# Causal term of the row maxima as row-half products, with new tables of times

## The chip, the cores and the metric

The kernel runs on one core of one Trainium2 chip. The metric is the device time of one execution in microseconds (us); lower is better. The engines are PE (TensorE matmul; PEld is its weight load), DVE (VectorE), ACT (ScalarE), POOL (GpSimd) and SP (the queue that issues DMAs). They run asynchronously and meet at semaphores; each takes its own instructions strictly in program order.

## The reference, cut to what matters

Eight sequences of 512 tokens with 256 channels pass through two layers. Each layer is attention and a feed-forward part, each with layernorms and a residual. Layer 0's attention has 16 heads of 16 channels with rotary positions:

```python
q = apply_rope(split(x @ Wq.T + bq)); k = apply_rope(split(x @ Wk.T + bk)); v = split(x @ Wv.T + bv)
att = jnp.einsum('bhqd,bhkd->bhqk', q, k) / scale
att = jnp.where(tril, att, -jnp.inf)
att = jax.nn.softmax(att, axis=-1)
y = jnp.einsum('bhqk,bhkd->bhqd', att, v) @ Wo.T + bo
...
h = jax.nn.silu(gate) * up            # feed-forward of layer 0, hidden 768
```

Layer 1 has 16 heads of 64 channels, a soft clamp `50 * tanh(sim / 50)` in place of row maxima, and a feed-forward of the form `sigmoid(r) * (relu(k)**2 @ W_v)` on a mix of each token with the one before.

## The kernel before

**Two phases.** `phase1` does layer 0 for all eight sequences, `phase2` layer 1; the last sequence of phase 1 overlaps the first of phase 2. Matrices are kept as a high and a low part of 32-bit words, so most products are three matmuls (`product`, L340).

**The order.** A sequence is cut into pieces ("rope 1", "max 4 0", "exp 3 2"). A dictionary `table` in each phase gives each piece a time in slots; `Schedule` folds times at `SLOTS = 24`: `time // 24` says in which later iteration of the loop the piece runs, and `time % 24` its place in the iteration. Every engine runs those of the pieces that it has a function for, in the order of the places. So one iteration works on up to four sequences at once, and the tables alone decide what stands behind what on each engine. What a piece waits for is written in its function (semaphores). `loading_table`, `prologue_table` and `closing_table` place the weight loads and the pieces around the change of phase. The middle iterations (3 to 6) are a hardware loop; the others are written out.

**Row maxima of layer 0.** The softmax needs each row's maximum ahead of the exponentials. A pair `a` has two heads `e`, one in partitions 0 to 47 and one in 64 to 111 of `qT` and `kT`, so the two heads' products (L901) use the lower and the upper 64 rows of the array. `row_max` on PE computes pair `a` in three units `k`: key tile 3; tiles 2 and 0; tile 1 (`MAX_UNITS`), each into the two banks of a ring `ring_d` of two units. The causal term is then added: for each tile and head one matmul of the 128x128 bf16 identity with `causal` (0 or -1e30), which uses all 128 rows of the array (L905). DVE reduces the unit (L770, "rmax"), PE transposes four heads' maxima (L913, "maxT"), ACT copies them (L698), and SP places them as a 49th row of `qT` (L599, "maxima"). The `score` products (L929) run on 49 rows, also in row halves; their units are two single banks (`ring_s`) which the exponentials (ACT L708) free.

**Rotary chain.** PE "rope" (12 matmuls, L340), DVE "roped" (L761, L763), POOL "rope_sum" (L638), ACT "rope_hi" (L686), POOL "rope_lo" (L642), and then SP "place" (L592), six DMAs for each of four parts, which bring `roped` to `kT` or `qT`. "max 0 0" waits for places 0 and 1, "max 4 0" for 2 and 3. POOL also masks the probabilities ("mask", L216 and three L221) and forms low halves ("hidden_lo", L655).

**End of layer 0's attention.** "o" (PE), "o_out", "o_stats" and "o_norm" with the residual add (DVE L802, L316, L332, L815), "x1_stats", POOL "x1_rstd" (L328), DVE "x1_norm" (L332), and PE "x1_T" (L963), from which the feed-forward's gate and up products start.

**Phase 2.** PE's larger units alternate between the two halves of `ring_s` there: ... score 4 2, qk 6, r, key, score 5 0 ... A "qk" unit is read by ACT "qk_hi" (L1344) and then DVE "qk_lo" (L1424), which frees it; "r" is read and freed by ACT "r_out" (L1381). "key" takes the unit that "qk 6" held. Layer 1's probabilities are freed through "tanh" (ACT L1354). "den" and "recip" (DVE L1433) are the softmax denominators, "o" adds a pair into the output (L1589).

The places are floats. In phase 2 "r_out" stands at 40.48 and "qk_hi 6" at 16.48:

```python
self.order = sorted(times, key=lambda piece: times[piece] % length)
```

Of the kernel before, what the change touches and what calls it, by code (L numbers as in the profile page):

```python
# [66 lines left out]
class Schedule:  # L67
# [28 lines left out]
    def tail(self, length):  # L96

        return [(j * length + self.place[piece], piece, j - self.shift[piece]) for j in range(BATCH, self.last + 1)
                for piece in self.order if self.present(j, piece)]
# [256 lines left out]
def phase1(nc, block, ctx, memory, a, x_mid, tok, banks, psum, ident, expo):  # L356
# [40 lines left out]
    causal = sb("causal", [P, P], BF16)  # L397
    identb = sb("identb", [P, P], BF16)
# [14 lines left out]
    with nc.sbuf_tensor("l0_staging", [P, 2 * NM, T], F32, side="right") as raw:  # L413
# [30 lines left out]
        "maxT_out": {(0,): 7.28, (1,): 12.62, (2,): 18.46, (3,): 23.86},
        "maxima": {(0,): 8.17, (1,): 18.03, (2,): 21.23, (3,): 26.53},
        "pv": {(0,): 15.68, (1,): 21.44, (2,): 29.89, (3,): 33.35},
        "pv_out": {(0,): 15.89, (1,): 23.68, (2,): 29.21, (3,): 31.18},
        "outT": {(0,): 19.01, (1,): 24.9, (2,): 32.26, (3,): 33.65},
        "outT_norm": {(0,): 19.04, (1,): 24.56, (2,): 30.73, (3,): 33.23},
        "att_T": {(0,): 33.79, (1,): 34.01},  # L450
        "att_T_hi": {(0,): 33.24, (1,): 33.42},
        "att_T_lo": {(0,): 33.44, (1,): 33.6},
        "o": {(0,): 35.78, (1,): 35.99},
        "o_out": {(0,): 34.28, (1,): 34.92},
        "x1_T": {(0,): 40.07, (1,): 41.01},
        "x1_T_hi": {(0,): 39.85, (1,): 40.46},
        "x1_T_lo": {(0,): 40.83, (1,): 42.16},
        "o_stats": {(): 35.25},
# [1199 lines left out]
```

## Time and profile before

| | us |
|---|---|
| median of 3 runs (1732.78 to 1738.29) | 1736.45 |
| profiled execution | 1738.71 |
| its span, first to last instruction | 1737.0 |
| PE busy | 1556.6 |
| DVE / ACT / POOL busy | 1065.2 / 834.8 / 827.8 |
| mean granted TensorE clock, share of full | 0.932 |

Phase 2's first matmuls on PE stand at 797.4 us; in steady state an iteration of phase 1 takes 93.6 to 94.9 us and one of phase 2 some 106.3 us. A matmul's start is the number to trust: ends are modelled, so its cost is the distance from its start to the next one's. At 2.4 GHz 128 columns stream in 53 ns, 256 in 107 ns and 512 in 213 ns. The granted clock is 1.00 (2.4 GHz) or 0.50 (1.2 GHz).

### The profile page before, as it was taken

The page shows a single profiled execution, that of the slowest core. Times are in us where ns is not written, and L with a number is a line of the kernel's source. Part 1 is how long each engine was busy: PE and PEld are TensorE (multiplying, and loading weights), DVE is VectorE, ACT ScalarE, POOL GpSimd, SP SyncE. Part 2 cuts the span into 40 slices and gives each one's busy share as a digit, 9 for nine tenths or more (in the row PEclk, how much of TensorE's full clock was granted, in tenths as well). Part 3 has the DMA queues.
Part 4 walks back from the last instruction along what each step waited for, and adds up shares of the span by engine and source line. Part 5 has one row for each costly group of instructions (what it writes and reads, how often), then busy time and mean ns, then how long its engine had stood idle before and what let it go on. Part 6 is the DMA issues. An engine that isn't in the chain of part 4 may idle for free.

```text
span 1737.0 us, 28461 instructions
## 1 busy us (share of the span) xinstructions
PE 1556.6 (90%) x10528; PEld 1109.1 (64%) x10528; DVE 1065.2 (61%) x1796; ACT 834.8 (48%) x1205; POOL 827.8 (48%) x1007
## 2 busy tenths in 40 slices
PE   2788999999898999898999999999999999999963
PEld 2445675756666666666777677676776767767643
DVE  3557576676757676675565577565674656747562
ACT  2233444343433434364555566655666556655531
POOL 2132343334343424342455655766566556675552
PEclk9677999989999989998999999999999999999986
DMA  6433332222233332311010001010000100000000
GB/s 143 62 50 50 49 62 50 37 46 47 43 49 61 49 61 37 62 62 61 25 47 8 1 2 37 1 38 1 8 28 0 36 0 27 9 1 25 1 25 12
DMA packets 46768, 61.31 MB, mean 35 GB/s; under 512 B 4928, under 2 KB 31968, under 8 KB 46688
## 3 DMA queue, kind: packets, MB, share of 16 engines
q1 hardware_dynamic: 45824, 59.56, 16.9%
q8 instruction: 53, 0.87, 0.2%
q10 hardware_dynamic: 864, 0.66, 0.1%
q14 instruction: 27, 0.22, 0.1%
HBM read 26.35 MB, written 8.39 MB: 20 GB/s over the span
## 4 chain that ended last, share of the span: by engine, by line
PE 75%; ACT 5%; issue 5%; DVE 5%; POOL 4%; DMA 4%; SPq 2%; POOLq 0%; ACTq 0%; DVEq 0%
PE psum L340 36%; PE psum L1573 8%; PE psum L1548 7%; PE psum L1589 5%; PE psum L943 4%; PE psum L929 4%; PE psum L1561 4%; DMA l_qT<-l_roped_hi 2%; PE psum L901 2%; SPq L592 2%; PE psum L905 2%; ACT l_probs L708 2%; ACT l_probs L1354 1%; PE psum L963 1%; POOL l_roped_lo L642 1%
## 5 line engine op out<-in xcount | busy, mean ns | idle before, releaser
L708 ACT ACTIVATE l_probs<-psum 128x512 f32<-128x512 f32 (+1 forms) x384 | 181.0, 524 | 291.0 <-PE psum L929 290.3
L1433 DVE RECIPROCAL l_att<-psum 128x512 f32<-128x512 f32 x64 | 214.5, 3352 | 62.8 <-PE psum L1561 60.7
L770 DVE TENSOR_REDUCE l_rowmax<-psum 128x2 f32<-128x1024 f32 (+3 forms) x256 | 203.0, 819 | 79.9 <-PE psum L905 78.8
L1354 ACT ACTIVATE l_probs<-psum 128x1024 f32<-128x1024 f32 (+1 forms) x192 | 165.0, 879 | 112.5 <-PE psum L1548 84.3
L1424 DVE TENSOR_TENSOR l_qk_lo<-psum,l_qk_hi 128x1024 fp32r<-128x1024 f32 x64 | 78.0, 1220 | 200.6 <-ACT l_qk_hi L1344 200.6
L221 POOL TENSOR_SCALAR_AFFINE_SELECT l_probs<-l_probs 128x256 f32<-128x256 f32 (+1 forms) x384 | 182.6, 507 | 0.0
L216 POOL TENSOR_TENSOR l_pool_holder<-expo 128x1 f32<-128x1 f32 x128 | 28.8, 225 | 292.5 <-ACT l_probs L708 183.2
L1360 ACT ACTIVATE l_probs<-l_probs 128x2048 f32<-128x2048 f32 (+1 forms) x128 | 160.8, 1269 | 1.6
L1573 PE MATMUL psum<-l_probs,l_v 128*64 128x512 f32 (+3 forms) x1024 | 150.4, 436 | 0.9 <-DVE l_att L1439 0.9
L1573 PEld LDWEIGHTS psum<-l_probs,l_v 128*64 128x64 f32 x1024 | 71.1, 137 | 89.6 <-issue 78.6
L929 PE MATMUL psum<-l_qT,l_kT 49*128 49x512 f32 (+3 forms) x512 | 100.8, 432 | 30.6 <-ACT l_probs L708 24.9
L1288 POOL TENSOR_TENSOR l_keysum<-l_probs 128x768 f32<-128x768 f32 x64 | 118.0, 1844 | 6.3
L901 PE MATMUL psum<-l_kT,l_qT 48*128 48x512 f32 (+3 forms) x512 | 86.9, 378 | 33.4 <-DMA l_qT<-l_roped_hi 26.6
L1296 POOL TENSOR_TENSOR l_attT_lo<-l_att,l_attT_hi 128x512 fp32r<-128x512 f32 x64 | 87.8, 1377 | 51.5 <-ACT l_attT_hi L1372 51.5
L328 POOL TENSOR_TENSOR l_x_rstd<-l_x_veps,expo 128x4 f32<-128x4 f32 x48 | 49.7, 1035 | 125.3 <-DVE l_x_veps L322 124.5
L655 POOL TENSOR_TENSOR l_hT_lo<-l_gated,l_hT_hi 128x512 fp32r<-128x512 f32 x48 | 61.5, 1282 | 98.9 <-ACT l_hT_hi L722 98.7
L638 POOL TENSOR_TENSOR l_roped_lo<-l_straight,l_turned 128x512 f32<-128x512 f32 x32 | 41.0, 1280 | 132.7 <-DVE l_turned L763 126.9
L1344 ACT ACTIVATE l_qk_hi<-psum 128x1024 fp32r<-128x1024 f32 x64 | 65.7, 1026 | 79.3 <-PE psum L340 78.9
L1548 PE MATMUL psum<-l_qk_hi 64*128 64x512 f32 (+3 forms) x512 | 97.6, 376 | 4.9 <-DVE l_qk_lo L1424 1.6
L943 PE MATMUL psum<-l_probs,l_v 128*32 128x512 f32 (+3 forms) x1024 | 92.5, 510 | 1.9 <-ACT l_probs L708 1.2
L929 PEld LDWEIGHTS psum<-l_qT,l_kT 49*128 49x128 f32 x512 | 47.2, 201 | 73.0 <-ACT l_probs L708 31.0
L901 PEld LDWEIGHTS psum<-l_kT,l_qT 48*128 48x128 f32 x512 | 51.2, 213 | 56.5 <-issue 44.4
(193 smaller groups left out, 4253.6 us busy)
## 6 DMA issues: line engine op xcount, KB each, us to landing
l_kT<-l_roped_hi SPq DMA_DIRECT2D x64, 128.0 KB, 4.0
l_qT<-l_roped_hi SPq DMA_DIRECT2D x64, 128.0 KB, 5.1
l_xin<-in_x SPq DMA_DIRECT2D x8, 512.0 KB, 4.2
l_kT<-l_roped_lo SPq DMA_DIRECT2D x32, 128.0 KB, 5.1
l_qT<-l_roped_lo SPq DMA_DIRECT2D x32, 128.0 KB, 4.7
l_x<-in_x SPq DMA_DIRECT2D x8, 512.0 KB, 4.0
x_mid<-l_x SPq DMA_DIRECT2D x8, 512.0 KB, 5.3
l_xin<-x_mid SPq DMA_DIRECT2D x8, 512.0 KB, 4.1
```

The source lines that it names most:

```text
L221: nc.gpsimd.affine_select(out=part, in_=part, compare_op=ALU.is_ge, fill=0.0, base=0, pattern=[[0, part.shape[1]], [1, P]], channel_multip ...
L340: last = nc.tensor.matmul(out, l(c), r(c), start=(k == 0), stop=(k == len(todo) - 1))
L708: ring_s.free(nc.scalar.activation(probs[:, SLOT[p], e, c0:c1], ring_s.unit(*use)[:, 0:c1 - c0], ACT.Exp, scale=HD0 ** -0.5), *use)
L770: reduced = nc.vector.tensor_reduce(rowmax[:, t, a // 2, :, a % 2], ring_d.unit("max", a, k)[:, :, c0:c0 + (t + 1) * P], mybir.AxisListTyp ...
L901: nc.tensor.matmul(unit[:, e, c0:c0 + (t + 1) * P], qT[rows, a, t * P:(t + 1) * P], kT[rows, a, 0:(t + 1) * P], start=(c0 == 0), stop=False)
L929: last = nc.tensor.matmul(ring_s.unit("score", p, u, e)[:, c0:c0 + T - kt * P], kT[rows, p, kt * P:(kt + 1) * P], qT[rows, p, kt * P:T], s ...
L943: last = nc.tensor.matmul(ring_d.unit("pv", g)[32 * j:32 * j + 32, 0, kt * P:T], v0[:, kt, h * VSTEP:h * VSTEP + 32], probs[:, SLOT[p], j ...
L1354: ring_s.free(nc.scalar.activation(probs[:, p % 2, :, c0:c1], ring_s.unit("score", p, u)[:, :, 0:c1 - c0], ACT.Tanh, scale=HD1 ** -0.5 / C ...
L1360: nc.scalar.activation(part, part, ACT.Exp, scale=CLAMP).then_inc(exped.sem, 1)
L1433: ring_d.free(nc.vector.reciprocal(att[p % 2][:], ring_d.unit("den", p)), "den", p)
L1548: last = nc.tensor.matmul(ring_s.unit("score", p, u)[:, e, c0:c0 + T - kt * P], l[half, slot, 1, kt * P:(kt + 1) * P], r[half, slot, 0, kt ...
L1573: last = nc.tensor.matmul(ring_d.unit("pv", p)[64 * e:64 * e + 64, kt * P:T], v1[:, kt, 2 * p + e, :], probs[:, p % 2, e, OFF1[kt]:OFF1[kt ...
```

## The change

1. The causal term of a tile and head is now two products of 64 rows each. Head `e` uses the row half of the array in which its own product runs. For `h = 0` the operands are the first 64 rows' selector and 128 columns, for `h = 1` the second 64 rows' selector and the last 64 columns only (the first 64 hold zeros there). The constants are `later` and `rows_of` in place of `causal` and `identb`, and POOL builds them with some more small operations at the start, which PE waits for.
2. All tables have new times, so pieces stand in another order on every engine, in both phases, and at the start and the change of phase.
3. Places are rounded to three decimals when compared, so that equal places count as equal.

```diff
-        self.order = sorted(times, key=lambda piece: times[piece] % length)
-        self.place = {piece: time % length for piece, time in times.items()}
+        self.place = {piece: round(time % length, 3) for piece, time in times.items()}
+        self.order = sorted(times, key=self.place.get)
...
-        for eye in (ident, identb):
...
+        for h in range(2):
+            eye = rows_of[:, h, ROW0 * h:ROW0 * h + ROW0]
+            nc.gpsimd.affine_select(out=eye, in_=eye, compare_op=ALU.not_equal, fill=1.0, base=0,
+                                    pattern=[[-1, ROW0]], channel_multiplier=1).then_inc(consts, 1)
+        nc.gpsimd.affine_select(out=later[:], in_=later[:], compare_op=ALU.is_ge, fill=MASKED, base=-ROW0,
+                                pattern=[[-1, P]], channel_multiplier=1).then_inc(consts, 1)
...
             for t, c0 in MAX_UNITS[k]:
-                for e in range(2):
-                    last = nc.tensor.matmul(unit[:, e, c0 + t * P:c0 + (t + 1) * P], identb[:], causal[:],
-                                            start=False, stop=(t == MAX_UNITS[k][-1][0]))
+                for h in range(2):
+                    for e in range(2):
+                        rows = slice(ROW0 * e, ROW0 * e + ROW0)
+                        c1 = c0 + t * P
+                        last = nc.tensor.matmul(unit[:, e, c1 + ROW0 * h:c1 + P], rows_of[rows, h, :], later[rows, 0:P - ROW0 * h],
+                                                start=False, stop=(t == MAX_UNITS[k][-1][0] and h == 1))
...
-        "rope_lo": {(0,): -5.62, (1,): -1.8, (2,): 0.82, (3,): 9.75},
+        "rope_lo": {(0,): -8.13, (1,): -4.93, (2,): 7.35, (3,): 11.37},
```

PE, where the written-out first iteration computes maxima (`l_kT,l_qT` is the product of queries and keys, L901 before and L913 after). Before:

```order
L901 MATMUL psum<-l_kT,l_qT 128x512 x2
L905 MATMUL psum<-l_causal,l_identb 128x128 x2
L901 MATMUL psum<-l_kT,l_qT 128x384 x2
L901 MATMUL psum<-l_kT,l_qT 128x128 x2
L905 MATMUL psum<-l_causal,l_identb 128x128 x4
```

After:

```order
L913 MATMUL psum<-l_kT,l_qT 128x512 x2
L920 MATMUL psum<-l_later,l_rows_of 128x128 x2
L920 MATMUL psum<-l_later,l_rows_of 128x64 x2
L913 MATMUL psum<-l_kT,l_qT 128x384 x2
L913 MATMUL psum<-l_kT,l_qT 128x128 x2
L920 MATMUL psum<-l_later,l_rows_of 128x128 x2
```

Each pair of full-array matmuls became two pairs in row halves, 64 columns shorter in all, and nothing between the two heads' products uses the full array.

POOL in the loop of phase 1, from the end of "rope_sum 0" on (L638 and L650 are "rope_sum", L642 and L654 "rope_lo", L216 and L221 the masks, L655 and L667 "hidden_lo"; REGISTER_ALU and ISA rows are its waits and loop counters). Before, from behind mask 2:

```order
L150 REGISTER_ALU
L216 TENSOR_TENSOR l_pool_holder<-expo 128x1
L221 AFFINE_SELECT l_probs<-l_probs 128x4x128
L221 AFFINE_SELECT l_probs<-l_probs 128x2x128 x2
L641 ISA
L642 TENSOR_TENSOR l_roped_lo<-l_roped_lo,l_roped_hi 128x512
L654 ISA
L655 TENSOR_TENSOR l_hT_lo<-l_gated,l_hT_hi 128x512
L150 REGISTER_ALU
L638 TENSOR_TENSOR l_roped_lo<-l_straight,l_turned 128x512
L641 REGISTER_ALU
L642 TENSOR_TENSOR l_roped_lo<-l_roped_lo,l_roped_hi 128x512
```

After, from behind mask 2:

```order
L653 ISA
L654 TENSOR_TENSOR l_roped_lo<-l_roped_lo,l_roped_hi 128x512
L150 REGISTER_ALU
L650 TENSOR_TENSOR l_roped_lo<-l_straight,l_turned 128x512
L653 REGISTER_ALU
L654 TENSOR_TENSOR l_roped_lo<-l_roped_lo,l_roped_hi 128x512
L150 REGISTER_ALU
L216 TENSOR_TENSOR l_pool_holder<-expo 128x1
L221 AFFINE_SELECT l_probs<-l_probs 128x4x128
L221 AFFINE_SELECT l_probs<-l_probs 128x2x128 x2
L666 ISA
L667 TENSOR_TENSOR l_hT_lo<-l_gated,l_hT_hi 128x512
```

"mask 3" and "hidden_lo 0" moved from ahead of "rope_sum 1" and "rope_lo 1" to behind them.

ACT in phase 2 (L1360 and L1375 are the exponentials, L1381 and L1396 "r_out", L1344 and L1359 "qk_hi 6"). Before:

```order
L1360 ACTIVATE l_probs<-l_probs 128x2x1024
L1354 ACTIVATE l_probs<-psum 128x2x256
L1360 ACTIVATE l_probs<-l_probs 128x2x256
L1381 ACTIVATE l_sig_r<-psum 128x1024
L1344 ACTIVATE l_qk_hi<-psum 128x1024
L1395 ACTIVATE l_dx<-psum 128x1024
```

After:

```order
L1369 ACTIVATE l_probs<-psum 128x2x256
L1375 ACTIVATE l_probs<-l_probs 128x2x1024
L1359 ACTIVATE l_qk_hi<-psum 128x1024
L1375 ACTIVATE l_probs<-l_probs 128x2x256
L1396 ACTIVATE l_sig_r<-psum 128x1024
L1410 ACTIVATE l_dx<-psum 128x1024
```

"qk_hi 6" stood behind "r_out" and now stands ahead of it. Other orders of which the prediction speaks, as piece names: on PE of phase 1 "o 0, o 1, score 0 2, score 1 0, max 4 0, maxT 1, score 1 1, score 1 2, max 4 1, score 2 0, max 4 2, pv 0, max 5 0, x1_T 0" became "o 0, score 0 2, o 1, max 4 0, score 1 0, maxT 1, max 4 1, score 1 1, score 1 2, score 2 0, max 4 2, max 5 0, pv 0, x1_T 0"; on DVE there "rmax 4 1, x1_stats, rmax 4 2" became "rmax 4 1, rmax 4 2, x1_stats"; ahead of it "x2_norm, rmax 3 2, outT_norm 3" became "outT_norm 3, x2_norm, rmax 3 2". "gate 3" moved from ahead of "max 0 0" on PE to behind it. On DVE of phase 2 "qk_lo 1, recip 6" became "recip 6, qk_lo 1".

## Rows read from the trace of the kernel before

**Rows 1.** The page, part 1: busy us (share of the span) xinstructions.
```profile
PE 1556.6 (90%) x10528; PEld 1109.1 (64%) x10528; DVE 1065.2 (61%) x1796; ACT 834.8 (48%) x1205; POOL 827.8 (48%) x1007
```

**Rows 2.** Waits of PE: who waited <- for whom: us in total, times, longest.
```profile
PE psum L901 <- DMA l_qT<-l_roped_hi: 26.6, 7, 12.5
...
PE psum L340 <- DVE l_qk_lo L1424: 23.0, 7, 3.3
```

**Rows 3.** Windows of phases 1 and 2: us, busy times, PEclk, DMA share, GB/s.
```profile
0.00:797.30 797.30, 695.25 (x4752) 474.84 (x4753) 504.06 (x1009) 310.54 (x618) 282.67 (x413) 0.90 0.31 57
797.30:1683.20 885.90, 846.62 (x5710) 621.00 (x5708) 541.54 (x735) 516.56 (x579) 534.38 (x587) 0.98 0.05 17
```

**Rows 4.** Timeline, PE, phase 1: start us, us, instruction, count.
```profile
311.08 0.29 PE L905 MATMUL psum<-l_causal,l_identb 128*128 128x128 bf16 x2
311.29 0.50 PE L929 MATMUL psum<-l_qT,l_kT 49*128 49x512 f32 x2
311.63 0.40 PE L901 MATMUL psum<-l_kT,l_qT 48*128 48x384 f32 x4
311.97 0.40 PE L905 MATMUL psum<-l_causal,l_identb 128*128 128x128 bf16 x4
312.17 0.47 PE L340 MATMUL psum<-l_yT_hi,l_wgu_hi 128*128 128x512 f32 x1
312.49 0.39 PE L340 MATMUL psum<-l_yT_lo,l_wgu_hi 128*128 128x512 f32 x1
```

**Rows 5.** Timeline, PE, phase 2: 64-row pairs of 128 columns.
```profile
1088.07 0.27 PE L1548 MATMUL psum<-l_qk_lo,l_qk_hi 64*128 64x128 f32 x2
1088.18 0.28 PE L1548 MATMUL psum<-l_qk_hi,l_qk_lo 64*128 64x128 f32 x2
```

**Rows 6.** Timeline, 471 to 492 us: POOL, SP's queue and PE.
```profile
471.32 1.35 POOL L221 TENSOR_SCALAR_AFFINE_SELECT l_probs<-l_probs 128x512 f32<-128x512 f32 x3
...
479.45 1.27 POOL L638 TENSOR_TENSOR l_roped_lo<-l_straight,l_turned 128x512 f32<-128x512 f32 x1
481.46 1.29 POOL L642 TENSOR_TENSOR l_roped_lo<-l_roped_lo,l_roped_hi 128x512 fp32r<-128x512 f32 x1 [0.74 <-ACT l_roped_hi L686]
...
485.31 1.24 SPq L592 DMA_DIRECT2D l_qT<-l_roped_hi  x2
...
491.58 0.50 PE L901 MATMUL psum<-l_kT,l_qT 48*128 48x512 f32 x2 [2.14 <-DMA l_qT<-l_roped_hi]
```

**Rows 7.** Windows of one iteration of phase 1.
```profile
440.90:456.70 15.80, 12.63 (x96) 7.45 (x94) 13.58 (x38) 6.15 (x14) 5.01 (x10) 0.78 0.33 77
...
492.50:499.30 6.80, 6.80 (x24) 4.67 (x22) 2.94 (x4) 1.09 (x2) 0.00 (x0) 0.50 0.00 0
```

**Rows 8.** Timeline, DVE and PE, phase 1, around x1_norm and x1_T.
```profile
454.04 0.69 DVE L770 TENSOR_REDUCE l_rowmax<-psum 128x2 f32<-128x512 f32 x1
455.25 1.38 DVE L332 TENSOR_SCALAR l_gated<-l_x,l_x_mv,l_x_rstd 128x256 f32<-128x256 f32 x4 [0.51 <-POOL l_x_rstd L328]
...
456.68 0.55 PE L963 MATMUL psum<-ident,l_gated 128*128 128x128 f32 x3
```

**Rows 9.** Timeline, PE, ACT and DVE, phase 2, around the r and key products.
```profile
1093.71 0.28 PE L340 MATMUL psum<-l_wrkv_hi,l_mixr_hi 128*128 128x256 f32 x1
...
1096.71 1.02 ACT L1381 ACTIVATE l_sig_r<-psum 128x1024 f32<-128x1024 f32 x1 [2.63 <-PE psum L340]
1097.63 1.02 ACT L1344 ACTIVATE l_qk_hi<-psum 128x1024 fp32r<-128x1024 f32 x1
...
1098.68 1.22 DVE L1424 TENSOR_TENSOR l_qk_lo<-psum,l_qk_hi 128x1024 fp32r<-128x1024 f32 x1 [8.95 <-ACT l_qk_hi L1344]
...
1099.96 0.71 PE L340 MATMUL psum<-l_mixk_hi,l_wrkv_hi 128*128 128x512 f32 x1 [3.29 <-DVE l_qk_lo L1424]
```

**Rows 10.** Window in phase 2 behind such a wait.
```profile
994.30:997.70 3.40, 3.40 (x10) 2.66 (x9) 0.00 (x0) 0.00 (x0) 3.05 (x3) 0.50 0.01 2
```

**Rows 11.** The page, part 5: busy, mean ns | idle before.
```profile
L1433 DVE RECIPROCAL l_att<-psum 128x512 f32<-128x512 f32 x64 | 214.5, 3352 | 62.8 <-PE psum L1561 60.7
```

More of the change, by code:

```diff
@@ L96, in tail @@
     def tail(self, length):
-        return [(j * length + self.place[piece], piece, j - self.shift[piece]) for j in range(BATCH, self.last + 1)
+        return [(round(j * length + self.place[piece], 3), piece, j - self.shift[piece]) for j in range(BATCH, self.last + 1)
                 for piece in self.order if self.present(j, piece)]
@@ L444, in phase1 @@
[L444 to L458, printed above, removed]
-        "o_rstd": {(): 36.56},
-        "residual": {(): 38.86},
-        "o_norm": {(): 36.73},
-        "x1_stats": {(): 37.93},
-        "x1_rstd": {(): 38.53},
-        "x1_norm": {(): 39.85},
@@ new lines, in phase1 @@
+        "outT_norm": {(0,): 19.48, (1,): 26.58, (2,): 29.43, (3,): 32.25},
+        "att_T": {(0,): 34.44, (1,): 34.91},
+        "att_T_hi": {(0,): 34.22, (1,): 34.27},
+        "att_T_lo": {(0,): 33.91, (1,): 34.01},
+        "o": {(0,): 35.92, (1,): 36.13},
+        "o_out": {(0,): 35.03, (1,): 35.9},
+        "x1_T": {(0,): 40.2, (1,): 40.82},
+        "x1_T_hi": {(0,): 40.73, (1,): 41.84},
+        "x1_T_lo": {(0,): 40.66, (1,): 41.21},
+        "o_stats": {(): 36.14},
+        "o_rstd": {(): 37.27},
@@ new lines, in phase1 @@
+        "residual": {(): 36.14},
+        "o_norm": {(): 36.23},
+        "x1_stats": {(): 37.12},
+        "x1_rstd": {(): 38.61},
+        "x1_norm": {(): 40.18},
+        "gate": {(0,): 41.86, (1,): 43.76, (2,): 47.77, (3,): 49.04, (4,): 50.8, (5,): 52.38},
+        "tanh": {(0,): 43.53, (1,): 46, (2,): 47.98, (3,): 48.46, (4,): 51.47, (5,): 54.61},
+        "gated": {(0,): 43.67, (1,): 44.96, (2,): 48.09, (3,): 50.92, (4,): 52.12, (5,): 53.01},
+        "up": {(0,): 42.82, (1,): 44.58, (2,): 48.63, (3,): 50.4, (4,): 51.73, (5,): 53.54},
@@ L499, in start @@
     def start(pieces):
-        timed = sorted([*times.items(), *loading.items()], key=lambda entry: entry[1] % SLOTS)
+        timed = sorted([*times.items(), *loading.items()], key=lambda entry: round(entry[1] % SLOTS, 3))
         for piece, _ in timed:
@@ L1116, in phase2 @@
[L1116 to L1125 removed]
+        "load_x": {(): -15.66},
+        "x_stats": {(): -17.44},
+        "x_rstd": {(): -16.12},
+        "x_norm": {(): -4.47},
+        "x_T": {(0,): -2.88, (1,): -2.61},
+        "x_T_hi": {(0,): -1.68, (1,): -1.05},
@@ L1126, in phase2 @@
+        "mix_lo": {(0,): 37.82, (1,): 38.28},
+        "r": {(): 41.13},
+        "r_out": {(): 40.72},
+        "key": {(): 41.73},
+        "key_out": {(): 41.26},
+        "square": {(): 43.59},
+        "kact_hi": {(): 44.18},
+        "kact_lo": {(): 47.02},
+        "out": {(): 44.93},
+        "out_out": {(): 46.29},
+        "gate": {(): 45.21},
+        "x4_stats": {(): 47.67},
+        "x4_rstd": {(): 52.11},
+        "x4_norm": {(): 52.53},
+        "store": {(): 49.62},
     }
```

251 lines of the change are left out of this document (119 added, 132 removed).

## The prediction

> **What bounds the kernel now.** I read the page's busy times first [rows 1]: PE is busy for 90% of the span, the next engine, DVE, for 61%. So I asked in which stretches PE is not the limit. The windows by phase [rows 3] say: phase 1 has PE busy for 695 of 797 us at a mean clock of 0.90, phase 2 for 847 of 886 us at 0.98. There is thus some slack in phase 1, and next to none in phase 2 beyond single waits. The waits of PE [rows 2] name two that the change of order touches: 26.6 us for the DMAs that place the rotated queries (12.5 us of it once, at the start) and 23.0 us, in seven waits of 3.3 us, for DVE's "qk_lo" of phase 2. The rest of the time PE works, so matmuls that get cheaper count nearly in full, unless another chain sets the end of the stretch in which they stand.
>
> **The causal products.** The timeline of PE [rows 4] prices them from start to start. Four L905 with 128 columns take 0.20 us (311.97 to 312.17), 0.05 us each, which is just their columns. What surrounds them costs more. Going from the row halves to the full array: the four L901 at 311.63 have 512 columns in all (0.213 us) and the next starts 0.34 us later, 0.13 us extra; I use 0.11, since not every such step comes out as dear. Going back: the two L905 at 311.08 need 0.107 us, the next starts 0.21 us later, 0.10 us extra. The first 32-bit pair after such a change is late once more: 311.29 to 311.63 is 0.34 us for 512 columns (0.213 us), 0.12 us extra. A full-array product behind L905 pays only on its first step: 312.17 to 312.49 is 0.32 us, 0.10 us over its columns.
>
> An iteration of phase 1 has 24 maximum units with 32 tiles. Before: 24 entries at 0.11 (2.6 us), 64 matmuls at 0.053 (3.4 us), 11 units followed by another row-half product at 0.22 (2.4 us), 13 followed by something else at 0.10 (1.3 us); 9.7 us. After: entry is free. The new pairs run in no row of this trace. Their lower bound is a bf16 step of the full array, 0.055 us a pair (the two heads run at once, as L901's do); the upper bound is the nearest pair in row halves, 32-bit and 128 columns, 0.11 us [rows 5]. I take 0.055 us, since the weights are bf16 like L905's: 64 pairs, 3.5 us. The 64-column pair gets no more than that credit, since four instructions stand behind each pair. In the new order 13 units are followed by row halves (0.09 us each for the next pair's 32-bit weights, 1.2 us) and 11 by something else (now a change, 0.21 us each, 2.3 us). Sum 7.0 us. The new order also has six more changes elsewhere (score products cut in between full-array ones): 6 x 0.21 = 1.3 us. Net gain 1.4 us an iteration, 11 us over eight. Four of the 24 units stand in a stretch that PE does not end (below), so I book **-10 us**. At 0.11 us a pair this term would be +17 us.
>
> The Trainium skill, "TensorEngine Tiling (Array Packing)", section Instruction Overhead, states about 60 cycles of overhead for each matmul and the same latency for 1 column as for 60. That speaks against the change: with 64 matmuls more in an iteration it would be an estimate of 0.025 us x 64 x 8 = 13 us more, and the term +3 instead of -10. The rows show no such overhead on four L905 in a row, so my sum goes without it.
>
> **The wait at "max 0 0".** Without the 12.5 us at the start it is 26.6 - 12.5 = 14.1 us in six waits [rows 2], one an iteration from the third sequence on. The timeline [rows 6] shows the chain: POOL does mask 3 (471.32) and hidden_lo 0 before rope_sum 1 at 479.45, and rope_lo 1 ends at 482.75; then six DMAs leave, the last pair from 485.31; PE goes on at 491.58, 6.3 us later, after 2.14 us of waiting, so it was there at 489.4. In the new order rope_sum 1 and rope_lo 1 stand right behind rope_lo 0. Input for rope_sum 1 was ready by 466.4; with rope_lo 0 at some 469.7 the pair is done at about 473.5. SP then becomes the limit: maxima 2 and twelve DMAs at 0.62 us from about 471.5 end at 480; the last pair then leaves at 478.8, and with the same 6.3 us it has landed by 485.1. PE arrives 1.4 us earlier than now ("gate 3" has moved behind, its work is only postponed) and about 1 us earlier through cheaper masks: 487. The wait goes, with 2 us to spare: **-12 us**, leaving 2 for iterations where it does not.
>
> **The clock behind it.** After this wait the granted clock is 0.50 for 3.4 or 6.8 us, with PE busy all the time [rows 7]; over these six places 23.9 us ran at 1.2 GHz, which costs half of that, 12 us. Without the idle time before it I expect most of it back: **-9 us**.
>
> **What gets worse in phase 1.** From o 0 to x1_T 0 (440.90 to 456.68) PE is busy for 12.6 of 15.8 us, at a mean clock of 0.78, and DVE for 13.6 [rows 7]. x1_norm ends at 456.6 and x1_T starts at 456.68 [rows 8]: the norm chain through DVE sets this stretch, PE only just keeps up. The new order makes that chain longer: o 1 comes behind score 0 2 and two changes of mode (0.5 us), and rmax 4 2 (0.69 us [rows 8]) ahead of x1_stats: +1.2 us. The same stretch starts earlier, because outT_norm 3 no longer waits behind x2_norm and rmax 3 2: the wait of 0.9 us ahead of att_T goes, 0.7 us net. Sum +0.5 us in seven iterations: **+3.5 us**. PE will stand idle ahead of x1_T instead of ahead of scores, and the clock drop there stays; it costs nothing while the norms are late.
>
> **The wait at "key" in phase 2.** [rows 9]: qk 6 has ended at 1093.71 when r starts. ACT takes r_out first, at 1096.71, and only at 1097.63 qk_hi 6; qk_lo 6 follows at 1098.68, ends at 1099.90, and key starts at 1099.96, after 3.29 us of waiting. The tables tie here (16.48 twice) and the float remainder decides. In the new order qk_hi 6 stands ahead of r_out. ACT is free by then (tanh 4 2 and the exponential fit into the 4.2 us of o 0 and qk 6), so qk_hi 6 and qk_lo 6 take 1.02 + 1.22 us from 1093.71, done at 1096.1, before r's last matmul at 1096.5. The wait is gone, seven times: **-23 us**. What is late next is "out", whose operands come 1 us before PE by my walk through the chain key, square, kact.
>
> Behind each of these waits the clock falls to 0.50 for 3.4 us (once 6.8) [rows 10], 27.3 us in all, 13.6 us lost. No other drop stands in phase 2's steady state. **-12 us**.
>
> **What gets worse in phase 2.** Its new order has 38 changes of array mode instead of 35 in an iteration: 3 x 0.21 x 7 = **+4.4 us**. And DVE does recip 6 (3.35 us [rows 11]) before qk_lo 1 (1.22 us): 4.7 us from den 6's end until score 0 1 may start, against 4.1 us of PE's work in between (o 4, pv 6, score 0 0, den 7): 0.6 us; x3_T comes 0.8 us closer to the norm that it waits for: at most as much again. 1.2 x 7: **+8 us**. The start and the last 54 us keep their chains: 0. POOL's extra constants (eight small operations of 0.3 us) fit into its 11.5 us of idle time before x_rstd; without that cover they would cost 2 us once.
>
> **Sum.** -10 - 12 - 9 + 3.5 - 23 - 12 + 4.4 + 8 = -50 us, against 1738.7 us of the profiled execution: 1688.6. That execution is 2.3 us over the median of the runs: 1686. I forecast 1685 us.
>
> **Rivals.** *Only phase 2 gains (14 in 100).* For it: phase 1 has 100 us of slack on PE, and the norm chain may set more of an iteration than the one stretch. Then -23 - 12 + 12 = -23 us: 1713. *Row-half pairs go at the pace of 32-bit weights (10 in 100).* For it: the only 64-row rows [rows 5]; against it: bf16 L905 at 0.05. 27 us more than the forecast: 1712. *The wait at key goes elsewhere (6 in 100):* DVE or POOL, 60% busy, come late at den or score by as much; phase 1's -27 stays: 1709 to 1720. *Nothing of the order's gains comes (4 in 100):* both waits are replaced, and the masks' gain pays for the added changes: within 5 us of before. *Slower: half-filled arrays do not hold the clock (5 in 100).* The causal products were the only full-array work inside the runs of maxima and scores. If PE's clock stays at 1.2 GHz through these runs, an iteration of phase 1 would have some 20 us more at half speed, 10 us lost, 80 us in all against the 50 gained: 1765. It decides from 12 us more at half clock in an iteration. Against it: scores and L901 run at full clock between 456.7 and 489.4.
>
> **The numbers.** The forecast itself has 61 in 100, with its own range of 1664 to 1702: phase 2's +8 may be 0, the clock may come back in full and the masks be dearer or cheaper by 10. The range to 1714 takes in the first three rivals in part and leaves out about 2 in 10. A change under 0.3% (5 us) can't be told from none. Faster 0.90, same 0.04, slower 0.06.
>
> **What would show it.** In the changed profile: no wait of PE for "qk_lo" ahead of key and no 0.50 clock behind it; an iteration of phase 2 near 102.5 us; no DMA wait at max 0 0; an idle PE of 2 to 4 us ahead of x1_T; L920 pairs 0.05 to 0.06 us apart; an iteration of phase 1 near 90.5 us. I am wrong if L920 pairs stand 0.1 us apart, if the windows of phase 1 show more half clock, or if a new wait of over 2 us stands in each iteration.

## The result, and the profile after

The changed kernel takes 1665.47 us (median of 4 runs, 1663.48 to 1669.93) against 1737.37 us; the ratio of the means is 0.9594, 95% interval [0.9567, 0.9621]. The forecast was 1685 us with a range of 1662 to 1714, and faster at 90 in 100. So the direction and the range hold, though the time stands only 3.5 us above the range's lower end, and the gain is 72 us where 51 were forecast (profiled execution against profiled execution: 1666.4 against 1738.7, and 1688.6 forecast). The missing 22 us are the subject below.

The page's busy times of the changed kernel, as in [rows 1]:

```profile
PE 1517.2 (91%) x11040; PEld 1090.6 (66%) x11040; DVE 1068.6 (64%) x1796; ACT 833.4 (50%) x1205; POOL 834.3 (50%) x1012
```

PE has 512 matmuls more and 39 us less busy time. Its waits (who waited <- for whom, us in total, times, longest), as in [rows 2]:

```profile
PE psum L944 <- ACT l_probs L720: 23.5, 26, 1.2
...
PE psum L913 <- DMA l_qT<-l_roped_hi: 12.5, 1, 12.5
...
PE psum L913 <- DVE l_rowmax L782: 9.7, 12, 1.7
```

Of the seven DMA waits of [rows 2] only the first one, at the start, is left, and the wait for "qk_lo" ahead of key has gone from the list. The waits of the maximum products for DVE's reductions have grown from 2.3 us to 9.7. The windows, as in [rows 3], with phase 2 now starting at 757.7 us, and the last row the closing chain:

```profile
0.00:757.70 757.70, 666.75 (x5265) 464.55 (x5266) 500.45 (x1009) 312.75 (x618) 285.36 (x418) 0.92 0.34 60
757.70:1610.50 852.80, 835.44 (x5709) 612.50 (x5707) 548.61 (x735) 513.02 (x578) 538.24 (x587) 0.99 0.06 18
1610.50:1664.60 54.10, 15.03 (x69) 13.58 (x68) 19.55 (x52) 7.68 (x9) 10.72 (x8) 0.59 0.04 15
```

Phase 1 ends 39.6 us earlier (797.3 to 757.7; the forecast's terms for it sum to -27.5), and what follows is 32.8 us shorter (forecast -22.6). An iteration of phase 1 takes 88.5 to 88.8 us from x1_T to x1_T (92.1 to 95.1 in the kernel before, measured the same way; forecast near 90.5), one of phase 2 102.0 from key to key (forecast near 102.5).

The timeline of PE where a row-half causal term stands between other row-half products, as in [rows 4]:

```profile
383.87 0.50 PE L913 MATMUL psum<-l_kT,l_qT 48*128 48x512 f32 x2
384.22 0.26 PE L920 MATMUL psum<-l_later,l_rows_of 64*128 64x128 bf16 x4
384.31 0.48 PE L944 MATMUL psum<-l_qT,l_kT 49*128 49x512 f32 x2
384.63 0.40 PE L913 MATMUL psum<-l_kT,l_qT 48*128 48x384 f32 x4
```

The four L920 of a tile (a pair of 128 columns and a pair of 64) take 0.09 us from start to start (384.22 to 384.31), and 192 columns stream in 0.080. So a tile costs less than the 0.11 us of the forecast and far less than the 0.22 of its upper bound. The next pair of 512 columns takes 0.32 us (384.31 to 384.63), 0.11 us over its columns: that part of the step back to 32-bit operands stayed, as the forecast had it (0.09). The Trainium skill's "TensorEngine Tiling (Array Packing)", section Instruction Overhead, states some 60 cycles of overhead for each matmul. Taken as time that each matmul adds, as in the prediction's estimate, the trace does not agree: 192 columns leave 0.01 us over, for two pairs. Taken as the least time of a matmul, as in the section's example (1 column takes as long as 60), these rows say nothing of it, since both products have more columns than that.

Around key in phase 2, as in [rows 9] (PE, ACT and DVE):

```profile
1047.18 0.28 PE L340 MATMUL psum<-l_wrkv_hi,l_mixr_hi 128*128 128x256 f32 x1
...
1047.38 1.03 ACT L1359 ACTIVATE l_qk_hi<-psum 128x1024 fp32r<-128x1024 f32 x1
...
1048.44 1.23 DVE L1439 TENSOR_TENSOR l_qk_lo<-psum,l_qk_hi 128x1024 fp32r<-128x1024 f32 x1 [5.70 <-ACT l_qk_hi L1359]
...
1049.98 0.40 PE L340 MATMUL psum<-l_mixk_hi,l_wrkv_hi 128*128 128x512 f32 x1
```

qk_hi 6 starts 0.2 us after r, qk_lo 6 ends at 1049.67, and key starts at 1049.98 without a wait.

### The profile page after: what moved, and what is told of

Same layout as the page of the kernel before. It is cut to its first block, busy times and chain, and to the rows that moved or that the text cites. A ratio compares the mean times of both kernels' runs of the same rounds, so it can differ in the third digit from the quotient of the medians.

```text
span 1664.6 us, 29499 instructions
## 1 busy us (share of the span) xinstructions
PE 1517.2 (91%) x11040; PEld 1090.6 (66%) x11040; DVE 1068.6 (64%) x1796; ACT 833.4 (50%) x1205; POOL 834.3 (50%) x1012
## 4 chain that ended last, share of the span: by engine, by line
PE 83%; DVE 8%; ACT 3%; issue 2%; POOL 2%; DMA 2%; SPq 1%; POOLq 0%; DVEq 0%; ACTq 0%
PE psum L340 41%; PE psum L1588 8%; PE psum L1563 8%; PE psum L1604 5%; PE psum L958 5%; PE psum L1576 4%; PE psum L944 4%; PE psum L913 3%; DVE l_rowmax L782 2%; PE psum L920 1%; ACT l_probs L1369 1%; PE psum L978 1%; ACT l_probs L720 1%; PE psum L967 1%; PE psum L928 1%
## 5 line engine op out<-in xcount | busy, mean ns | idle before, releaser
L221 POOL TENSOR_SCALAR_AFFINE_SELECT l_probs<-l_probs 128x256 f32<-128x256 f32 (+1 forms) x384 | 180.6, 502 | 0.0
L1375 ACT ACTIVATE l_probs<-l_probs 128x2048 f32<-128x2048 f32 (+1 forms) x128 | 160.1, 1270 | 1.3
L216 POOL TENSOR_TENSOR l_pool_holder<-expo 128x1 f32<-128x1 f32 x128 | 29.2, 228 | 243.3 <-ACT l_probs L720 121.8
L1311 POOL TENSOR_TENSOR l_attT_lo<-l_att,l_attT_hi 128x512 fp32r<-128x512 f32 x64 | 93.7, 1469 | 61.4 <-ACT l_attT_hi L1387 61.2
L944 PE MATMUL psum<-l_qT,l_kT 49*128 49x512 f32 (+3 forms) x512 | 96.8, 415 | 25.7 <-ACT l_probs L720 23.5
L913 PE MATMUL psum<-l_kT,l_qT 48*128 48x512 f32 (+3 forms) x512 | 88.0, 384 | 27.7 <-DMA l_qT<-l_roped_hi 12.5
L667 POOL TENSOR_TENSOR l_hT_lo<-l_gated,l_hT_hi 128x512 fp32r<-128x512 f32 x48 | 61.8, 1287 | 90.0 <-ACT l_hT_hi L734 90.0
L650 POOL TENSOR_TENSOR l_roped_lo<-l_straight,l_turned 128x512 f32<-128x512 f32 x32 | 41.1, 1285 | 130.7 <-DVE l_turned L775 125.0
L1359 ACT ACTIVATE l_qk_hi<-psum 128x1024 fp32r<-128x1024 f32 x64 | 65.8, 1028 | 77.1 <-PE psum L340 77.1
L913 PEld LDWEIGHTS psum<-l_kT,l_qT 48*128 48x128 f32 x512 | 50.6, 207 | 54.2 <-issue 32.4
L1305 POOL TENSOR_TENSOR l_keysum<-l_keysum,l_probs 128x512 f32<-128x512 f32 x64 | 83.4, 1303 | 5.0
```

The lines of the kernel that those rows point to most:

```text
L221: nc.gpsimd.affine_select(out=part, in_=part, compare_op=ALU.is_ge, fill=0.0, base=0, pattern=[[0, part.shape[1]], [1, P]], channel_multip ...
L913: nc.tensor.matmul(unit[:, e, c0:c0 + (t + 1) * P], qT[rows, a, t * P:(t + 1) * P], kT[rows, a, 0:(t + 1) * P], start=(c0 == 0), stop=False)
L944: last = nc.tensor.matmul(ring_s.unit("score", p, u, e)[:, c0:c0 + T - kt * P], kT[rows, p, kt * P:(kt + 1) * P], qT[rows, p, kt * P:T], s ...
L1375: nc.scalar.activation(part, part, ACT.Exp, scale=CLAMP).then_inc(exped.sem, 1)
```

## The experiments

Times are medians of 5 or 6 runs; the kernel before had medians of 1737.4 to 1738.2 us beside them. The changed kernel was not run again beside them; differences to it are differences to its median of 1665.5 us.

**One tie undone.** The kernel before, one number changed.

```diff
-        "qk_hi": {..., (5,): 14.69, (6,): 16.48, (7,): 20.03},
+        "qk_hi": {..., (5,): 14.69, (6,): 16.47, (7,): 20.03},
```

> The kernel before, with one place of phase 2 changed: qk_hi 6 at 16.47 instead of 16.48, so that ACT takes it ahead of r_out. My theory: this one swap is the whole of phase 2's gain. The seven waits of 3.29 us ahead of key go and with them the seven drops of the clock behind them (23.8 us at half, 12 us lost): 33 to 38 us less than before, some 1700 us, and a key-to-key distance of 101.4 us instead of 106.3. Rival: the gain of phase 2 needs the whole new order; the swap alone moves the wait to out or to the scores behind it and brings 5 to 15 us.

1703.2 us, ratio 0.9796 [0.9775, 0.9816]: 34.3 us less, as the theory had it (33 to 38; the terms were 23 + 12). Windows of one iteration and of the whole of phase 2's middle:

```profile
1092.50:1193.79 101.29, 100.82 (x702) 73.75 (x701) 66.55 (x92) 63.97 (x71) 66.78 (x73) 1.00 0.05 17
821.30:1598.59 777.29, 771.32 (x5293) 566.03 (x5293) 496.67 (x670) 482.75 (x540) 499.50 (x548) 1.00 0.05 17
```

The clock is 1.00 over 777 us. Nearly half of what the change brings comes from a tie in the table that a float remainder had decided the wrong way.

**The tie put back.** The changed kernel with "qk_hi 6" at 16.73, behind "r_out" (16.72).

> The changed kernel with one place of phase 2 moved: qk_hi 6 behind r_out, as before. Theory: the wait of 3.3 us ahead of key comes back in each of the seven iterations, and behind it 3.4 us at half clock: +33 to +38 us over the changed kernel (1700). Rival: in the new order another piece covers it, +0 to +12 us; or the wait comes back but the clock stays up, since nothing else in the iteration waits: +23 us.

1696.7 us, 31 us over the changed kernel, just under the theory's 33 to 38. The wait of 3.29 us is back seven times, but the drop of the clock only four times: none stands behind the first, the second and the last wait. Windows behind the second, the fourth, the fifth and the last of these waits:

```profile
1054.65:1058.10 3.45, 3.45 (x18) 2.59 (x20) 0.00 (x0) 0.35 (x1) 3.18 (x3) 1.00 0.00 0
1268.22:1271.60 3.38, 3.38 (x8) 2.73 (x9) 0.00 (x0) 0.00 (x0) 3.14 (x4) 0.51 0.00 0
1375.26:1380.70 5.44, 5.44 (x14) 3.86 (x14) 0.00 (x0) 0.00 (x0) 3.81 (x3) 0.50 0.00 0
1590.60:1594.00 3.40, 3.40 (x18) 2.56 (x20) 0.00 (x0) 0.32 (x1) 3.18 (x3) 1.00 0.00 0
```

**Row-half causal products alone.** The kernel before with the change's part 1, all orders as they were.

> The kernel before with the row-half causal products (and their constants) alone, all orders as before. Theory: the products are cheaper by themselves. By the prediction's terms 2.7 us an iteration without the six extra changes of mode (9.7 to 7.0), less what falls where PE doesn't set the end: -18 us. With the pair spacings that the changed kernel's trace shows (67 ns for 128 columns, 28 for 64, nothing extra behind them) 3.5 us an iteration: -25 us. The DMA wait at max 0 0 stays at about 2 us or grows, since PE arrives earlier. Rival A: the earlier arrival of PE at its waits swallows the gain: 0 to -8 us. Rival B: more instructions cost more than they save: +3 to +13 us.

1723.1 us, ratio 0.9913 [0.9899, 0.9926]: -14.4 us, between the theory's 18 and rival A's 8, and well short of the 25 that the pair spacings gave.

**Full-array products in the new order**, the reverse: the changed kernel with the causal term as before.

> The changed kernel with the causal term as before (full-array identity times causal), in the new order. Theory: as in the old order the full-array form costs 2.7 to 3.5 us an iteration more, and 13 instead of 11 units are followed by a row-half product (0.4 us): +20 to +30 us over the changed kernel. Rival A: the new order brings nearly all of the gain and the form of the products matters little: +0 to +8. Rival B: the clock drops again once the full-array products stretch the gaps, +40 or more.

1685.2 us, 20 us over the changed kernel. So the products are worth 14 us in the old order and 20 in the new. Windows from x1_T of the first sequence to that of the seventh (six iterations): before (first), with the row-half products alone (second), the changed kernel (third). Columns as in [rows 3].

```profile
173.66:738.53 564.87, 524.64 (x3688) 364.76 (x3689) 372.60 (x759) 226.20 (x454) 215.05 (x305) 0.94 0.29 50
```

```profile
170.92:725.89 554.97, 507.18 (x4073) 364.42 (x4073) 372.03 (x759) 226.23 (x454) 216.21 (x305) 0.94 0.30 51
```

```profile
168.49:700.22 531.73, 501.44 (x4072) 354.36 (x4073) 371.86 (x758) 227.82 (x454) 219.67 (x305) 0.96 0.33 53
```

In the old order PE's busy time falls by 17.5 us (524.64 to 507.18), 2.9 us an iteration, but the window by 9.9 only: PE's idle time grows from 40.2 to 47.8 us. PE arrives earlier and then waits for others. The wait at max 0 0 grew little, from 12.9 to 13.5 us over the six; the waits of the scores and of maxT for ACT's exponentials grew by 3.1 us together, and 2.7 us are new in which pv (the products of probabilities and values) waits for POOL's masks.

**Each causal product twice.** The changed kernel with every L920 issued two times (the term is added twice, which changes no result).

> The changed kernel with each causal product issued twice in a row (adding -1e30 once more changes no result): 64 more pairs an iteration, 32 of 128 and 32 of 64 columns. Theory, from the pair spacings in the changed kernel's trace (67 ns and 28 ns): 32 x 0.095 = 3.0 us an iteration, +24 us in all, less the part in the stretch of the norms: +20 to +24. At the pace of 32-bit rows (0.11 us a pair) it would be +56; at the 25 ns of fixed cost a pair over the columns, +30 to +38.

1696.7 us, +31.3 us, where the spacing of the rows asked for 20 to 24. That lies in the range which the expectation gave for a fixed cost of 25 ns a pair (+30 to +38), so the starts have to decide:

```profile
308.39 0.35 PE L920 MATMUL psum<-l_later,l_rows_of 64*128 64x128 bf16 x8
308.57 0.37 PE L944 MATMUL psum<-l_qT,l_kT 49*128 49x256 f32 x2
```

A doubled tile takes 0.18 us to the next product, where 384 columns are 0.16 us and four pairs at 25 ns more would make 0.26. So the fixed cost is not there. The window over the six iterations:

```profile
170.25:730.42 560.17, 523.11 (x4841) 375.42 (x4841) 372.53 (x759) 228.06 (x454) 217.82 (x305) 0.95 0.31 51
```

Busy time grows by 21.7 us, 3.6 an iteration for 64 pairs (3.0 by the spacing; the rest is most likely the lower clock, 0.95 for 0.96), and idle time by 6.8. Three waits of 3.0 us stand ahead of score products (384.0, 480.6 and 575.1 us) that the changed kernel doesn't have; the profile names no cause for them, and behind two of the three the clock drops to 0.50. So a longer PE path also brought waits and clock drops back. The price of a pair is near its columns; the price of an iteration isn't the sum of pairs.

**POOL's order alone.** The kernel before with the two places that the prediction held responsible for the DMA wait.

```diff
-        "mask": {..., (3,): 17.46, ...},
+        "mask": {..., (3,): 22.25, ...},
...
-        "hidden_lo": {(0,): 42.8, ...},
+        "hidden_lo": {(0,): 46.26, ...},
```

> The kernel before with two places of POOL in phase 1 moved: mask 3 and hidden_lo 0 behind rope_lo 1, as in the changed kernel; masks, tables and phase 2 else as before. Theory: the chain POOL, SP, DMA ends before PE arrives, the 2.1 us of waiting ahead of max 0 0 go in each iteration (-10 to -14 us in all) and with them the second drop of the clock (24 us at half, -12): -20 to -24 us, some 1715. Rival A: PE meets the same wait a little later (maxima 2 or probabilities of mask 3 come late): 0 to -6. Rival B: the wait goes but the clock falls all the same: -12.

1746.1 us, ratio 1.0045 [1.0031, 1.0060]: slower by 9 us. The theory fell, and rival A names the place. The timeline of ACT, POOL and PE:

```profile
384.63 0.63 ACT L686 ACTIVATE l_roped_hi<-l_roped_lo 128x512 fp32r<-128x512 f32 x1
385.35 1.28 POOL L642 TENSOR_TENSOR l_roped_lo<-l_roped_lo,l_roped_hi 128x512 fp32r<-128x512 f32 x1 [9.12 <-ACT l_roped_hi L686]
...
390.17 1.26 POOL L642 TENSOR_TENSOR l_roped_lo<-l_roped_lo,l_roped_hi 128x512 fp32r<-128x512 f32 x1 [2.29 <-ACT l_roped_hi L686]
...
391.53 1.35 POOL L221 TENSOR_SCALAR_AFFINE_SELECT l_probs<-l_probs 128x512 f32<-128x512 f32 x3
...
392.93 3.90 PE L943 MATMUL psum<-l_probs,l_v 128*32 128x512 f32 x32 [4.05 <-POOL l_probs L221]
```

rope_lo 0 waits 9.12 us for ACT's rope_hi 0, and mask 3, now behind rope_lo 1, comes 4.05 us late for pv 1. The clock drops behind that wait as it did behind the DMAs': it is 0.50 over 392.90 to 396.10 us. Of the waits of PE, the one for the DMAs is down to the 12.5 us at the start and 0.9 more, and a longer one has come in its place:

```profile
PE psum L943 <- POOL l_probs L221: 29.8, 8, 4.3
...
PE psum L901 <- DMA l_qT<-l_roped_hi: 13.4, 2, 12.5
```

**ACT's places with them.** The same, and

```diff
-        "rope_hi": {(0,): -2.55, (1,): -0.93, ...},
+        "rope_hi": {(0,): -5.73, (1,): -2.09, ...},
```

> The experiment with POOL's order, and besides two places of ACT: rope_hi 0 ahead of exp 3 1 or so (-5.73) and rope_hi 1 at -2.09, as in the changed kernel. There rope_hi 0 starts 9.9 us behind x1_T 0, before 17.7 us, and rope_lo 1 (and so mask 3 behind it) can't be earlier than that allows. Theory: with both the whole chain is early enough, pv 1 doesn't wait for mask 3 and max 0 0 not for the DMAs: 10 to 14 us of waiting gone and half to all of the 12 us of clock: -12 to -24 us against before. Rival A: mask 3 still comes late for pv 1 by 1 to 3 us an iteration: within 5 us of before. Rival B: rope_hi on ACT delays the exponentials of the scores, +5.

1707.7 us, ratio 0.9821 [0.9804, 0.9838]: -30.5 us, more than expected. In its timeline of ACT and POOL, where x1_T 0 stands at 350.85, rope_hi 0 starts 12.3 us behind it, where POOL's order alone had 17.7 (384.63 from 366.96):

```profile
363.16 0.63 ACT L686 ACTIVATE l_roped_hi<-l_roped_lo 128x512 fp32r<-128x512 f32 x1
363.87 1.27 POOL L642 TENSOR_TENSOR l_roped_lo<-l_roped_lo,l_roped_hi 128x512 fp32r<-128x512 f32 x1 [3.67 <-ACT l_roped_hi L686]
...
369.35 1.27 POOL L642 TENSOR_TENSOR l_roped_lo<-l_roped_lo,l_roped_hi 128x512 fp32r<-128x512 f32 x1 [2.95 <-ACT l_roped_hi L686]
370.73 1.35 POOL L221 TENSOR_SCALAR_AFFINE_SELECT l_probs<-l_probs 128x512 f32<-128x512 f32 x3
```

Its six iterations:

```profile
168.86:710.72 541.86, 513.55 (x3689) 357.02 (x3689) 371.82 (x759) 224.95 (x454) 215.58 (x305) 0.96 0.32 52
```

23 us less than before: idle time 40.2 to 28.3 (-11.9), busy time -11.1 with the clock up from 0.94 to 0.96. From profiled execution to profiled execution the difference is 28.6 us: the window begins 4.8 us earlier (173.66 to 168.86), and 0.8 us lie behind it. Ahead of it the same wait of PE for the DMAs stood once at 4.58 us (at 121.95 us) and is now 1.04. Not all of the 4.8 us need be the change: with one tie undone, where phase 1 is the old one, the window begins at 171.7 us.

**Two orders on DVE put back** in the changed kernel: "recip 6" behind "qk_lo 1" (27.64 for 26.71), and "x1_stats" ahead of "rmax 4 2" (36.85 for 37.12).

> The changed kernel with recip 6 behind qk_lo 1 on DVE in phase 2, as before. The prediction had this order at up to 8 us with x3_T. Theory after the traces: no wait of PE stands at the first scores in the changed kernel, so 0 (-2 to +2 us). Rival: it hides in the scores' start, -4 us or more.

> The changed kernel with x1_stats ahead of rmax 4 2 on DVE in phase 1, as before. Theory: x1_norm ends 0.7 us earlier, but PE works at half clock up to x1_T and is not waiting for it: the pv 0 products end at the same time as x1_norm, and max 5 0 waits for the maxima of rmax 4 2 instead (ring_d): 0 to +4 us. Rival (the prediction's): the norm chain sets the stretch, -5 us.

The first: 1665.9 us, no difference; the wait that the prediction priced isn't there. The second: 1677.1 us, 11.6 us slower, beyond either expectation. Its timeline on DVE and PE:

```profile
433.99 1.40 DVE L316 BATCH_NORM_STATS2 l_x_stats<-l_x 128x6 f32<-128x256 f32 x4
...
435.94 1.82 DVE L782 TENSOR_REDUCE l_rowmax<-psum 128x2 f32<-128x512 f32 x2
436.87 4.49 PE L958 MATMUL psum<-l_probs,l_v 128*32 128x512 f32 x32 [1.76 <-DVE l_rowmax L782]
437.68 1.38 DVE L332 TENSOR_SCALAR l_gated<-l_x,l_x_mv,l_x_rstd 128x256 f32<-128x256 f32 x4
...
441.30 0.89 PE L978 MATMUL psum<-ident,l_gated 128*128 128x128 f32 x4
```

rmax 4 2 comes at 435.94 behind the statistics, pv 0, which takes the ring unit that it frees, waits 1.76 us for it, and x1_T stands 2.2 us behind the end of x1_norm (439.06). Over the run there are seven such waits of pv, 10.5 us in all, and none in the changed kernel. The kernel before, with x1_stats ahead of rmax 4 2 as here, has only one, of 0.3 us: there pv 0 stands ahead of max 5 0 and takes the other unit of the ring. So the place of rmax 4 2 belongs to PE's new order, and its 11.6 us are no gain over the kernel before. In the changed kernel the same stretch runs as the forecast had it (windows from o 0 to x1_T, and of the drop in it), as in [rows 7]:

```profile
417.75:434.32 16.57, 12.89 (x105) 7.25 (x103) 14.54 (x38) 6.59 (x14) 5.64 (x10) 0.79 0.34 76
427.00:433.90 6.90, 5.82 (x38) 2.32 (x42) 6.82 (x19) 1.29 (x3) 3.11 (x5) 0.51 0.00 0
```

```profile
432.89 1.38 DVE L332 TENSOR_SCALAR l_gated<-l_x,l_x_mv,l_x_rstd 128x256 f32<-128x256 f32 x4
...
434.32 0.66 PE L978 MATMUL psum<-ident,l_gated 128*128 128x128 f32 x4
```

x1_norm ends at 434.27 and x1_T starts at 434.32, so the norm chain and PE arrive together.

**Fewer changes of array mode.** The changed kernel with o 3 and o 1 moved out of runs of scores in phase 2 (27.2 for 25.92; 19.17 for 18.93), and the same with max 3 2 and up 4 moved in phase 1 (9.9 for 10.72; 52.03 for 51.73).

> The changed kernel with two places of PE in phase 2: o 3 behind score 7 2 instead of between score 7 1 and 7 2, o 1 behind score 5 2 instead of between 5 1 and 5 2. Three changes of array mode less an iteration. Theory: 3 x 0.21 us x 7 = -4.4 us (1661), since PE sets phase 2's pace. Rival: ACT's tanh of the scores comes later and PE waits instead, 0 or +3.

> The same two places and two more in phase 1: max 3 2 right behind score 0 1 instead of between att_T 0 and att_T 1, up 4 behind max 1 1 instead of between max 0 2 and max 1 0: four changes less an iteration there. Theory: 4 x 0.21 x 8 = -6.7 us more than with phase 2 alone: 1654. Rival: in phase 1 something else waits (DVE's maxima of unit 3 2 or hidden 4 come at another time) and the gain is nothing or a loss of 5 us.

1670.9 us and 1685.5 us: 5.4 and 20 us slower, where 4.4 and 11 less were expected. The first difference is small beside the spread of the runs (the two intervals overlap), so its windows have to show it. The waits of PE at the scores of phase 2, in the changed kernel and in the first of these two:

```profile
PE psum L1563 <- ACT l_probs L1369: 2.8, 8, 0.8
```

```profile
PE psum L1563 <- ACT l_probs L1369: 7.5, 24, 0.9
```

They grow by 4.7 us. One iteration of phase 2 from key to key, in the changed kernel and in this one:

```profile
1049.98:1151.96 101.98, 101.23 (x702) 74.05 (x701) 67.67 (x92) 63.47 (x71) 67.13 (x73) 1.00 0.05 17
```

```profile
1053.66:1156.18 102.52, 101.20 (x702) 73.98 (x701) 67.21 (x92) 63.46 (x71) 66.98 (x73) 1.00 0.05 17
```

Three changes less did not lower PE's busy time (101.2 in both), and the idle time grew by 0.5 us. The "o" products between two scores most likely had been doing their work while ACT freed the scores' unit. Why the busy time shows nothing of the three changes stays open. The second kernel shows where phase 1 lost:

```profile
PE psum L978 <- DVE l_rowmax L782: 10.9, 6, 1.9
```

att_T now waits 1.8 us an iteration for a reduction on DVE; that it is the one of max 3 2, which takes its ring unit earlier, I take from the order and did not test.

**A few places.** The kernel before with the row-half products and five places: qk_hi 6, mask 3, hidden_lo 0, rope_hi 0 and rope_hi 1, as in the diffs above.

> The kernel before with row-half causal products and five places moved (qk_hi 6; mask 3, hidden_lo 0, rope_hi 0, rope_hi 1), the rest of its tables as they were. Theory: the effects add up as measured or expected apart: -34 (qk_hi 6), -14 to -20 (masks), -12 to -24 (the chain to max 0 0): 1659 to 1677 us. Rival: the chain's part is nothing and masks then give 14: some 1689.

1658.4 us, ratio 0.9542 [0.9526, 0.9558]: 7 us faster than the changed kernel, whose interval lies apart from this one, and just under the theory's 1659 to 1677. The three effects measured apart sum to 34.3 + 30.5 + 14.4 = 79.2 us, and together they gave 79.8. Its windows of phase 1's six iterations and of phase 2's six (key to key):

```profile
165.08:697.67 532.59, 496.97 (x4076) 355.92 (x4072) 371.53 (x759) 224.80 (x454) 216.04 (x305) 0.96 0.32 53
949.86:1557.03 607.17, 604.68 (x4202) 442.78 (x4201) 397.27 (x542) 383.51 (x426) 400.21 (x439) 1.00 0.05 15
```

## Why the prediction was right, and where it was short

**Key and the clock behind it, -35 of -50.** Right in mechanism and size: -34.3 alone, 31 in the new order. It was read from [rows 9] and [rows 10] alone.

**Causal products.** Right by themselves: 9.7 to 7.0, 2.7 us an iteration, was forecast (the 7.0 counts the new order's neighbours; with the old ones the same terms give 2.5), and in the old order PE's busy time fell by 2.9. At 0.09 us a tile they are cheaper than the 0.11 taken, and the rival "pace of 32-bit weights" is dead. What the forecast didn't have is that their worth hangs on the waits around them: 14 us in the old order, 20 in the new.

**Changes of mode, +10 in phase 1 (+8 of it in the sum) and +4.4 in phase 2.** The step that failed, together with the clock's. In PE's busy time they do appear: over the six iterations the changed kernel has 501.4 us against 497.0 for the kernel with a few places, 4.5 us for its more broken order, and in phase 2 an iteration has 101.2 us against 100.8 with the tie alone undone, 0.4 of the 0.63 booked. But in phase 1 its idle time is 5.3 us less (30.3 against 35.6), and the window is 0.9 us shorter. The likely reading is that pieces between scores and maxima work while PE would otherwise wait for ACT or DVE, and the change of mode is paid out of that wait. Taking three away in phase 2 saved no busy time and brought 4.7 us of waits. I had booked each at its full 0.21 us as if PE waited for nothing.

**The wait at max 0 0, -12, and the clock, -9.** The wait went, and with it the drops behind it: -30.5 us with four places of the old order moved, where 21 were booked. The prediction read its 14.1 us as six waits, one an iteration. In the trace 5.4 us of them are two waits at the start (0.79 at 77.2 and 4.58 at 121.95 us), and only four of the six steady ones stand in that row; the profile puts the other two, at 208.5 and 681.0 us, as "issue", time in which it shows nothing that PE waited for:

```profile
PE psum L901 <- issue: 4.2, 2, 2.2
```

The six steady waits are thus 12.9 us, and that the -12 fits is partly luck. The 23.9 us at half clock stand behind five of them; behind the sixth, at 681.0 us, there is no drop. With the four places moved, idle time fell by 11.9 in six iterations, as forecast; the clock's 12 us, of which I held back 3, came nearly in full (busy time -11.1); and there were 4.8 us more ahead of these iterations, where I had not looked, 3.5 of them in the wait at 121.95. The cause as I wrote it was incomplete: I named POOL's and SP's queues, and taking "rope_lo 0 at some 469.7" for granted passed over ACT, on which rope_hi had to move too: in the kernel before rope_lo 0 starts at 475.08, right behind rope_hi 0 (474.37). POOL's order alone made the kernel 9 us slower.

**The norm chain, +3.5.** The stretch grew by 0.8 us (15.8 to 16.6) and the wait ahead of att_T shrank, near the forecast. But rmax 4 2 ahead of x1_stats, priced as 0.69 us lost, saves 11.6 us in the new order of PE: it frees the ring for pv 0. The 2 to 4 us of idle PE ahead of x1_T did not appear, for PE runs at half clock up to it and arrives just in time.

**New waits in phase 2, +8.** They are not there; recip's order makes no difference. What the new order of phase 2 costs, against the old one with the tie undone, is 0.8 us an iteration (102.0 for 101.2) and 2.8 us from the last key to the end (104.5 for 101.7), but it gains 4.0 us from the first matmul of phase 2 to the first key. These windows are the changed kernel's and that of the kernel with a few places:

```profile
757.70:947.70 190.00, 183.95 (x1185) 136.85 (x1184) 115.74 (x165) 108.83 (x126) 101.49 (x112) 0.98 0.08 27
```

```profile
755.90:949.86 193.96, 187.08 (x1199) 139.94 (x1197) 112.59 (x165) 109.97 (x127) 99.83 (x113) 0.97 0.08 27
```

All in all it costs 4 us (906.9 for 902.8 from there to the end), of the 12.4 booked for both terms.

**The sum.** By experiments: the tie -34.3, the chain to max 0 0 with the clock -30.5, the causal products -14.4, and all other places in the tables +7, together -72. (From profiled execution to profiled execution the +7 is 5.9: 1.8 by the end of phase 1, 757.7 for 755.9, and 4.1 behind it.) The forecast had -35, -21, and -10 for the products with the mode changes of phase 1, and +16 for the rest. Of its -10, the products were some -18 (2.7 us x 8 iterations, 20 of 24 units) and the mode changes +8. So it was 9 us short on the chain, 17 us too dear on what the broken order costs (+24 for +7), 4 us too hopeful on the products and 1 on the tie: 22 us in all. The range held although two terms were off by 9 and 17 us. Which of the other places of phase 1 help and which hurt was not taken apart further.

**The slower rival, 5 in 100.** It did not come. From x1_T to the next drop, with maxima and scores in row halves throughout, PE's clock in the changed kernel is 1.00:

```profile
434.30:515.80 81.50, 77.56 (x638) 56.78 (x634) 55.71 (x111) 37.04 (x74) 33.60 (x46) 1.00 0.37 58
```

## What to carry to other kernels

Price a wait together with what the clock loses behind it, but a change of array mode only where PE wouldn't have waited anyway: here taking pieces out from between two units of a short ring gained nothing in phase 2 and cost 15 us more in phase 1. Follow a late transfer back through every engine before moving a piece on one of them; here POOL's places alone lost 9 us, and with two of ACT's gained 30. When a whole table changes, try the few places that the waits point to by themselves: here five places gave 7 us more than the full tables, each with the new causal products.

## What the runs showed of the hardware

The same wait of 3.29 us, with PE at full clock ahead of it, was followed by no drop three times (clock 1.00 behind 948.8, 1054.65 and 1590.6) and by a clock of 0.50 to 0.51 four times, for 3.4 or 6.8 us, in one and the same execution. In the kernel before, the wait of 1.9 to 2.3 us at max 0 0 was followed by a drop five times of six. So the length of a wait alone did not decide whether the clock dropped. Two pairs of 64-row bf16 matmuls, of 128 and 64 columns, take 0.09 us together, and the step behind the first 32-bit pair that follows is still 0.11 us over its columns (384.31 to 384.63), though the mode doesn't change.
